# Two layer normalisations moved to ScalarE in the first phase of an attention and FFN block, with new instruction orders

## The reference

```python
mod = (silu(c) @ wmod).reshape(8, 6, 1, 256); sa, ca, ga, sb, cb, gb = ...
ga, gb = sign-preserving max(|g|, 0.25)
h = layernorm(x) * (1 + ca) + sa                 # (x - mean) / sqrt(var + 1e-5)
q, k = phi(h @ Wq.T + bq), phi(h @ Wk.T + bk)    # phi = elu + 1;  v = h @ Wv.T + bv
# causal linear attention, 16 heads of 16, for each token t:
#   num_t = q_t . sum_{s<=t} k_s v_s^T ;  den_t = q_t . sum_{s<=t} k_s + 1e-6
x = x + ga * ((num / den) @ Wo.T + bo)
h = layernorm(x) * (1 + cb) + sb
x = x + gb * ffn_block(h)     # two layers: windowed attention with rotary embedding, then a gated GELU FFN
```

## Time and profile before

| | us |
|---|---|
| median of 3 runs | 3326.53 |
| lowest, highest | 3323.44, 3328.26 |
| the profiled execution | 3325.04 |
| its span | 3323.2 |
| PE busy | 3176.3 (96%) |
| DVE busy | 2807.2 (84%) |
| POOL busy | 2515.7 (76%) |
| ACT busy | 2068.8 (62%) |
| granted TensorE clock, mean | 0.988 |

### The profile page before, as it was taken

How to read it: one execution, slowest core, us unless ns; L and a number is a source line. 1 busy time by engine, 2 the same in 40 slices (tenths; PEclk the granted TensorE clock), 3 DMA queues, 4 the chain that set the end, 5 groups by cost and what they waited for, 6 DMA issues and landing times.

```text
span 3323.2 us, 84307 instructions
## 1 busy us (share of the span) xinstructions
PE 3176.3 (96%) x25436; PEld 2433.4 (73%) x25436; DVE 2807.2 (84%) x8628; ACT 2068.8 (62%) x5116; POOL 2515.7 (76%) x2636
## 2 busy tenths in 40 slices
PE   5999999789999999999999999999999999999998
PEld 3666666457777777777777777777777777777777
DVE  5999999678888888888888888888888888888885
ACT  3555555346666666666666666666666666666664
POOL 3888888677777776777677777887878787878785
PEclk8999999889999999999999999999999999999999
DMA  6211111100000000000000001111111111111110
GB/s 223 68 45 43 44 44 43 37 15 24 24 24 24 24 24 24 24 24 23 24 24 24 24 25 34 36 37 37 36 37 36 37 38 35 38 35 40 34 42 30
DMA packets 153068, 124.98 MB, mean 38 GB/s; under 512 B 22580, under 2 KB 149032, under 8 KB 152368
## 3 DMA queue, kind: packets, MB, share of 16 engines
q1 hardware_dynamic: 146352, 110.67, 10.9%
q10 hardware_dynamic: 6272, 8.93, 0.9%
HBM read 77.51 MB, written 42.02 MB: 36 GB/s over the span
## 4 chain that ended last, share of the span: by engine, by line
PE 75%; DVE 12%; issue 8%; POOL 2%; ACT 1%; DVEq 1%; DMA 0%; SPq 0%; POOLq 0%; ACTq 0%
PE bank L540 26%; PE bank L736 17%; PE bank L744 10%; PE bank L547 7%; PE bank L709 7%; PE bank L688 5%; DVE shared L1055 2%; DVE a_den L1044 1%; DVE a_den L1042 1%; DVE z L1010 1%; DVE a_moments L999 1%; DVE a_moments L1075 1%; DVE shared L1036 1%; DVE gated L1070 1%; DVEq L362 1%
## 5 line engine op out<-in xcount | busy, mean ns | idle before, releaser
L540 PE MATMUL bank<-WQKV,xT 128*128 128x512 f32 x1536 | 745.9, 609 | 4.9 <-DVE rotary_work L1109 4.4
L1301 POOL TENSOR_TENSOR rnorm<-clamped,HALF 128x8 f32<-128x8 f32 x256 | 420.4, 1642 | 431.0 <-DVE clamped L1126 430.8
L736 PEld LDWEIGHTS bank<-zT,W 128*128 128x128 f32 x5632 | 661.6, 193 | 61.9 <-issue 59.6
L736 PE MATMUL bank<-zT,W 128*128 128x128 f32 x5632 | 673.8, 276 | 1.8 <-ACT zT L919 1.8
L1314 POOL TENSOR_TENSOR shared<-shared,share_of 128x512 f32<-128x512 f32 x512 | 543.6, 1080 | 89.9 <-DVE shared L1161 89.9
L905 ACT ACTIVATE shared<-shared,negmax 128x256 f32<-128x256 f32 x1024 | 507.4, 499 | 25.4 <-DVE negmax L1145 23.8
L540 PEld LDWEIGHTS bank<-WQKV,xT 128*128 128x128 f32 x1536 | 264.4, 192 | 215.3 <-issue 214.5
L1324 POOL TENSOR_TENSOR shared<-shared,IDENT 128x256 f32<-128x256 f32 x512 | 377.5, 757 | 0.0
L1308 POOL TENSOR_TENSOR qk<-qk,rnorm 128x512 f32<-128x512 f32 x256 | 289.1, 1129 | 103.7 <-DVE qk L1116 93.7
L1145 DVE CUSTOM_DVE_ANT_0 shared<-bank,MASK 128x256 f32<-128x256 f32 x1024 | 365.7, 419 | 0.1
L744 PEld LDWEIGHTS bank<-W,shared 128*128 128x128 f32 x1280 | 243.0, 190 | 90.8 <-issue 58.8
(11 more groups left out here) (141 smaller groups left out, 6788.8 us busy)
## 6 DMA issues: line engine op xcount, KB each, us to landing
X<-xl_rows SPq DMA_DIRECT2D x128, 128.0 KB, 2.2
X<-in_x SPq DMA_DIRECT2D x64, 128.0 KB, 2.1
x_tiles<-ax SPq DMA_DIRECT2D x64, 128.0 KB, 1.7
xl_rows<-axl SPq DMA_DIRECT2D x64, 128.0 KB, 1.7
XS<-xl_rows SPq DMA_DIRECT2D x128, 64.0 KB, 2.4
xm_rows<-X SPq DMA_DIRECT2D x128, 64.0 KB, 1.6
xs<-xm_rows SPq DMA_DIRECT2D x128, 64.0 KB, 1.8
xl_rows<-X SPq DMA_DIRECT2D x64, 128.0 KB, 1.7
```

The lines of the kernel that those rows point to most:

```text
L540: mm = nc.tensor.matmul(held(tile, key)[:, 0:cols], lhsT[c], rhs[c], start=(c == 0), stop=(c == len(lhsT) - 1))
L736: mm = nc.tensor.matmul(held(tile, key)[:, k * P:(k + 1) * P], W1[:, tile.l, c, at:at + P], zT[:, c], start=(c == 0), stop=(c == KC - 1))
L1301: G.tensor_tensor(rnorm[q][:], clamped[q][:], HALF[:].to_broadcast((P, LH)), ALU.pow).then_inc(done[f"root_{key}"], 1)
```

## The change

Both normalisations of phase A go from DVE (`tensor_scalar`: subtract, multiply) to ACT, as Identity with scale rstd and offset -mean * rstd. POOL computes that offset in `a_root`: it multiplies the mean by -1, raises the variance to -0.5 as before, waits for that, and multiplies the two. So the step gives two signals a tile instead of one. The epsilon 1e-6 of `a_queries` is added as a tensor of 16 equal elements instead of a scalar. Two constants are filled at the start. The orders of all five engines in phase A and the PSUM banks of phase A are new; phase L's are not changed.

```diff
 ORDER_A = {
-    "SP": [(0, "a_modulation"), (0, "a_load"), (4, "a_keep_x1"), (5, "a_store")],
-    "PE": [(2, "a_project_v"), (1, "a_project"), (2, "a_turn_q"), (3, "a_number"), (2, "a_sum"), (2, "a_score"), (3, "a_out"),
-           (0, "a_turn_z"), (1, "a_cum")],
-    "ACT": [(2, "a_keep_kphi"), (2, "a_keep_cum"), (2, "a_keep_q"), (3, "a_keep_o"), (1, "a_exp"), (2, "a_copy0"),
-           (2, "a_copy1"), (0, "a_affine")],
-    "DVE": [(2, "a_prod"), (2, "a_queries"), (4, "a_stats2"), (2, "a_value"), (0, "a_stats"), (1, "a_bias"), (4, "a_norm2"),
-           (0, "a_norm"), (2, "a_state"), (1, "a_phi"), (2, "a_mask2"), (2, "a_mask3"), (3, "a_gate")],
-    "POOL": [(4, "a_x1"), (5, "a_mod"), (4, "a_root2"), (0, "a_root"), (3, "a_add_state"), (0, "a_pre"), (2, "a_mask0"),
-           (2, "a_mask1")],
+    "SP": [(0, "a_modulation"), (0, "a_load"), (5, "a_store"), (4, "a_keep_x1")],
+    "PE": [(2, "a_cum"), (1, "a_project"), (4, "a_out"), (2, "a_turn_q"), (2, "a_sum"), (3, "a_number"), (2, "a_score"),
+           (0, "a_turn_z"), (1, "a_project_v")],
+    "ACT": [(3, "a_copy0"), (3, "a_copy1"), (2, "a_keep_kphi"), (5, "a_norm2"), (2, "a_keep_cum"), (2, "a_keep_q"),
+           (0, "a_norm"), (1, "a_exp"), (3, "a_keep_o"), (0, "a_affine")],
+    "DVE": [(3, "a_mask3"), (2, "a_value"), (2, "a_prod"), (2, "a_queries"), (0, "a_stats"), (1, "a_bias"), (4, "a_gate"),
+           (2, "a_state"), (4, "a_stats2"), (1, "a_phi"), (2, "a_mask2")],
+    "POOL": [(3, "a_mask0"), (3, "a_mask1"), (5, "a_mod"), (0, "a_root"), (4, "a_x1"), (0, "a_pre"), (4, "a_root2"),
+           (3, "a_add_state")],
 }
...
+            def a_norm(tile):                                       # on ACT
+                after(act, done["a_root"], tile, per=2)
+                after(act, filled["az"], tile, back=1)
+                nc.scalar.activation(az[:], xin[tile.s][:], ACT.Identity, scale=a_rstd[0][:], bias=a_offset[0][:]).then_inc(done["a_norm"], 1)
+            def a_norm2(tile):                                      # on ACT
+                after(act, done["a_root2"], tile, per=2)
...
+                nc.scalar.activation(axl[tile.s % 2][:], ax1[tile.s % 2][:], ACT.Identity, scale=a_rstd[1][:],
+                                     bias=a_offset[1][:]).then_inc(done["a_norm2"], 1)
...
-            def a_norm(tile):                                       # on DVE
...
-                V.tensor_scalar(az[:], xin[tile.s][:], a_meanvar[0][:, 0:1], a_rstd[0][:], ALU.subtract, ALU.mult).then_inc(done["a_norm"], 1)
...
-                V.tensor_scalar(a_den[:], a_den[:], EPS_DEN, None, ALU.add).then_inc(done["a_den"], 1)
+                V.tensor_tensor(a_den[:], a_den[:], EPSD[:], ALU.add).then_inc(done["a_den"], 1)
...
-            def a_norm2(tile):                                      # on DVE
...
-                V.tensor_scalar(axl[tile.s % 2][:], ax1[tile.s % 2][:], a_meanvar[1][:, 0:1], a_rstd[1][:], ALU.subtract,
-                                ALU.mult).then_inc(done["a_norm2"], 1)
...
             def a_root(k, tile):                                    # on POOL, for both normalisations
...
+                G.tensor_tensor(a_offset[k][:], a_meanvar[k][:, 0:1], MINUS[:], ALU.mult)
                 G.tensor_tensor(a_rstd[k][:], a_variance[k][:], HALF[:], ALU.pow).then_inc(done[("a_root", "a_root2")[k]], 1)
+                after(pool, done[("a_root", "a_root2")[k]], tile, per=2, ahead=-1)
+                G.tensor_tensor(a_offset[k][:], a_offset[k][:], a_rstd[k][:], ALU.mult).then_inc(done[("a_root", "a_root2")[k]], 1)
```

More of the change, by code:

```diff
@@ L81 @@
 BANK_A = {
-    "av": "20410305", "aqk": "63752641", "aq": "41031020", "num": "26475375", "kv": "63752641", "sc0": "04103752",
-    "sc1": "75264263", "sc2": "16375374", "sc3": "20410105", "awo": "10314204", "az": "16375265", "kphi": "75264763",
-    "cum": "16375224",
+    "kphi": "13041305", "cum": "26262616", "aqk": "30413042", "awo": "30413041", "aq": "57575747", "kv": "30413251",
+    "num": "26265626", "sc2": "75757674", "sc3": "13041305", "sc0": "26262416", "sc1": "04130723", "az": "30413042",
+    "av": "75757554",
 }
@@ L236, in adaln_block @@
         ZERO = sb("ZERO", [P, 1])
+        MINUS = sb("MINUS", [P, 1])
         modT = sb("modT", [P, B, 2 * KC])
@@ L246, in adaln_block @@
         a_variance, a_rstd = several(2, "a_variance", [P, 1]), several(2, "a_rstd", [P, 1])
+        a_offset = several(2, "a_offset", [P, 1])
+        EPSD = sb("EPSD", [P, AH])
         a_den, a_rden = sb("a_den", [P, AH]), sb("a_rden", [P, AH])
@@ L807, in _ @@
             last_project_a = {"a_project": "aqk", "a_project_v": "av"}[latest(ORDER_A["PE"], ["a_project", "a_project_v"])]
+            def a_norm(tile):
[4 more added lines that the diff above has]
+                after(act, done["a_root2"], tile, per=2)
+                if tile.least >= 2:
+                    n = (tile.s - 2) // STREAMS + 1
+                    act.wait_ge(stored[(tile.s - 2) % STREAMS], tile.at.block * (U * 4) + 16 * n)
+                nc.scalar.activation(axl[tile.s % 2][:], ax1[tile.s % 2][:], ACT.Identity, scale=a_rstd[1][:],
+                                     bias=a_offset[1][:]).then_inc(done["a_norm2"], 1)
             def a_affine(tile):
@@ L854, in a_keep_o @@
                 copy(flat(oaT), held(tile, "num")[:, 0:D]).then_inc(done["a_keep_o"], 1)
-            run_tiles(act, "A", ORDER_A["ACT"], {"a_affine": a_affine, "a_exp": a_exp, "a_keep_kphi": a_keep_kphi, "a_keep_cum": a_keep_cum,
+            run_tiles(act, "A", ORDER_A["ACT"], {"a_norm": a_norm, "a_norm2": a_norm2, "a_affine": a_affine, "a_exp": a_exp, "a_keep_kphi": a_keep_kphi, "a_keep_cum": a_keep_cum,
                                                  "a_keep_q": a_keep_q, "a_keep_o": a_keep_o,
@@ L952, in _ @@
             V.memset(HALF[:], -0.5).then_inc(consts_ready, 1)
+            V.memset(MINUS[:], -1.0).then_inc(consts_ready, 1)
+            V.memset(EPSD[:], EPS_DEN).then_inc(consts_ready, 1)
             V.memset(zeros, 0.0).then_inc(consts_ready, 1)
@@ L1003, in a_stats @@
                 after(dve, done["a_variance"], tile, per=3, ahead=-1)
-                after(dve, done["a_root"], tile, back=1)
+                after(dve, done["a_root"], tile, back=1, per=2)
                 V.tensor_scalar(a_variance[k][:], a_meanvar[k][:, 1:2], EPS_LN, None, ALU.add).then_inc(done["a_variance"], 1)
-            def a_norm(tile):
-                after(dve, done["a_root"], tile)
-                after(dve, filled["az"], tile, back=1)
-                V.tensor_scalar(az[:], xin[tile.s][:], a_meanvar[0][:, 0:1], a_rstd[0][:], ALU.subtract, ALU.mult).then_inc(done["a_norm"], 1)
             def a_bias(tile):
@@ L1079, in a_stats2 @@
                 after(dve, done["a_variance2"], tile, per=3, ahead=-1)
-                after(dve, done["a_root2"], tile, back=1)
+                after(dve, done["a_root2"], tile, back=1, per=2)
                 V.tensor_scalar(a_variance[1][:], a_meanvar[1][:, 1:2], EPS_LN, None, ALU.add).then_inc(done["a_variance2"], 1)
-            def a_norm2(tile):
[L1084 to L1087, removed]
-                V.tensor_scalar(axl[tile.s % 2][:], ax1[tile.s % 2][:], a_meanvar[1][:, 0:1], a_rstd[1][:], ALU.subtract,
-                                ALU.mult).then_inc(done["a_norm2"], 1)
-            steps = {"a_stats": a_stats, "a_norm": a_norm, "a_bias": a_bias, "a_value": a_value, "a_phi": a_phi, "a_prod": a_prod,
-                     "a_queries": a_queries, "a_state": a_state, "a_gate": a_gate, "a_stats2": a_stats2, "a_norm2": a_norm2}
+            steps = {"a_stats": a_stats, "a_bias": a_bias, "a_value": a_value, "a_phi": a_phi, "a_prod": a_prod,
+                     "a_queries": a_queries, "a_state": a_state, "a_gate": a_gate, "a_stats2": a_stats2}
             steps.update({f"a_mask{g}": partial(a_mask, g) for g in range(COPIED, GROUPS)})
```

2 lines of the change are left out of this document (1 added, 1 removed).

## The result

The changed kernel is slower: 3339.19 us (median of 6 runs, 3335.42 to 3341.40) against 3324.97 (6 runs of the kernel before, 3323.24 to 3328.26). The ratio is 1.0041, interval 1.0030 to 1.0052. The profiled execution took 3339.53 us, span 3337.7; that is 14.5 us over the span of before, at the same clock (0.987 and 0.988). Forecast were 3316 us.

What follows compares the result with a forecast made beforehand. PE and DVE were level at 9.03 us a tile in phase A, PE's own work 8.49. From 3325.04 us, 60 x (8.85 - 9.03) + 1.5 = -9.3 gave 3315.7, say 3316; range 3294 to 3338.

Steps and rivals of the forecast that it cites:

- A gate-to-gate period of 8.85 us: Phase A: the time from one tile's gate to the next was to fall from 9.03 to 8.85 us.
- well under 95%: Sign for 200 to 500 us: DVE busy well under 95%, with POOL over 92% and ACT near 70%.
- The small product: Each of four new one-element POOL products a tile was taken at 0.15 us from start to start.
- the 0.25 that I named as a sign of being wrong: The prediction called itself wrong if a one-element POOL product took over 0.25 us.
- POOL's case as a rival: Rival, chance 0.22: POOL becomes the bound; with 0.25 us a small product the period is 9.3 and the time 3343 us.
- The pause of PE at the turn of the queries: Phase A: PE waits 0 to 0.6 us a tile for the queries; half, 0.3, was taken, giving 8.8.
- just covered: `a_phi` was not to wait: `a_exp` ends some 3.2 us after the queries' turn, DVE's other work lasts about 3.5.
- 8.7 us of work and 0.2 of waiting a tile: POOL in phase A: 7.89 us own work plus 0.53 and 0.27 held by DVE, two idle waits of 0.1, giving 8.9.
- the epsilon at 0: L1044 as a tensor addition still waits for POOL: gain 0, bounds 0 and 0.57 us.
- the 1.37 us at four places, phase L (orders unchanged) and the DMAs [...] I cost at 0: Extra time where the program changes loop copies, phase L and the DMAs were all taken as unchanged, cost 0.
- POOL's slot without the rotary factors: POOL's per-tile sum in phase A: 7.05 us, 7.89 with new products and waits, 8.7 with what DVE holds.
- The filling and emptying at +1.5 (0 to 3): Phase A pipeline: `a_out` and `a_gate` a tile further back add a partly filled slot at the end, +1.5 us.

Runs made afterwards that it cites:

- experiment 9: Changed kernel with rotary factors multiplied before the first tile and 32 instructions of met waits in DVE's straight code between phase A's loops: 3323.47 us, ratio 0.9999.
- experiment 7: Changed kernel without POOL's two small offset products per root, ACT normalising with offset 0: 3324.54 us in a single run.
- Experiment 5: Kernel before with only the denominator's epsilon added as a tensor of 16 elements: 3324.31 us against 3324.03, ratio 1.0001.
- experiment 3: Changed kernel with met waits making 32 instructions on DVE ahead of its phase A: 3333.18 us, ratio 1.0024.
- 4: Changed kernel with met waits making 64 instructions on DVE ahead of its phase A: 3333.78 us, ratio 1.0030.
- experiment 2: Changed kernel with POOL multiplying the eight rotary factors before the first tile, not one by one in eight tiles: 3332.35 us, ratio 1.0024.
- experiment 1: Changed kernel with ACT issuing phase L's weight loads ahead of the first normalisation, not behind the affine step: 3337.85 us, ratio 1.0036.
- 10: Changed kernel with factors first, met waits between the loops, and the offset computed on ACT in place of POOL: 3325.28 us, ratio 1.0005.
- 8: Changed kernel with rotary factors first and met waits making 80 instructions on DVE ahead of its first tile: 3332.99 us, ratio 1.0024.
- 6: Changed kernel's new instructions in the kernel before's orders and banks, both normalisations on ACT ahead of the exponential: 3361.24 us, ratio 1.0105.
- 11: Changed kernel with rotary factors first and the product with -1 made by DVE ahead of the variance: 3324.53 us, ratio 0.9998.
- 12: Changed kernel with factors first, product with -1 on DVE, and 116 instructions of met waits in tiles 0 to 3: 3315.05 us, ratio 0.9969.

## Why the prediction was wrong

**Right: the slot and what bounds it.** "A gate-to-gate period of 8.85 us": 8.89 in undisturbed stretches. DVE was to be well under 95% and was 81%; POOL over 92%, and was 90% in a stretch that holds a hole (91.8% in experiment 9, which has none), a little short; ACT near 70%, and was 65%. The normalisations take 0.60 us each on ACT, where I took 0.55. The small product takes 0.19 us as reported and 0.14 from start to start (569.11 to 569.25 in POOL's timeline) where nothing holds it; 0.15 was taken. The first product's mean, 256 ns, is over the 0.25 that I named as a sign of being wrong; it comes from the 8 of 65 that wait out a DVE instruction (0.69 to 0.74 us; at 571.93 one takes 0.73, beside `a_phi`), and the other 57 are as forecast. POOL's case as a rival, a period of 9.3, didn't occur; the four products cost 0.14 a tile, by experiment 7.

The pause of PE at the turn of the queries was taken at 0.3 us a tile. PE's waits in the changed kernel, 200 to 500 us (us in total, times, longest), give 9.6 / 33 = 0.29, and another 0.17 for `a_phi`, which I had as just covered:

```profile
PE bank L550 <- DVE shared L1064: 9.6, 25, 0.8
PE bank L586 <- DVE LATE L1045: 5.6, 16, 0.6
```

POOL's part of the period is partly luck. I had 8.7 us of work and 0.2 of waiting a tile, 0.80 of the work for what DVE holds (0.53 and 0.27, which no row shows). In experiment 9 POOL is busy 275.6 of 300 us, 8.2 a tile, and idle 0.7: less work and more waiting, with nearly the same sum.

**Right: the epsilon at 0.** Experiment 5 measured 706 ns against 709. So by these rows the form with one SBUF input is held as well as the one with two.

**Wrong: what was costed at 0.** The step that failed is the one that read "the 1.37 us at four places, phase L (orders unchanged) and the DMAs [...] I cost at 0". I had seen the four places and taken them as a property of the loop. They are a property of where its code lies and how long it is. The change made DVE's body shorter (313 instructions in place of 352) and moved it: two jumps became free and two went to 4.5 us, which with the slower restart of PE cost 11.5 us. Against the 5.5 of before that is +6.0. Experiments 3 and 4 show it: they add nothing but met waits, and the holes went and came. Experiment 9 adds them to experiment 2, which by itself had kept both holes (4.38 and 4.25), and they went.

**Wrong: POOL's slot without the rotary factors.** I summed what POOL does in every tile, and left out what it does in eight of them, 1.28 us each. A slot in which POOL has room hides that; the change took the room, and the sum had to be made again for those tiles. By experiment 2 it is 6.8 us of the time.

**Wrong: the filling and emptying at +1.5 (0 to 3).** Experiment 9 is free of holes and factors, so it isolates the term. From the start to the first load of phase L it needs 630.23 us, 5.0 less than before. The slots alone would give 60 x (8.89 - 9.03) = -8.4, and the four jumps -5.5, together -13.9; so the filling and emptying cost about +9 net. I had also put the term at the end, and it lies at the start: the gate of tile 8 comes 9.8 us later than before (142.85 against 133.01), and from the gate of tile 56 to the first load of phase L it takes 2.6 us less (60.30 against 62.90). How much of it is the depth itself and how much ACT's DMA issues in the first eight tiles, stays open; experiment 1 moved those and got 1.1 us.

Phase L changed by +1.8 us, inside the 3 that were allowed. The sum with the measured terms, of the profiled executions: slots -8.4; jumps +6.0; the filling and emptying +8.9; phase L +1.8; and the factors +5.5, taken against experiment 9 like the filling (start to gate of tile 8: 146.00 against 142.85; tiles 24 to 40: 144.95 against 142.59). That is +13.8 where +14.5 was measured. Experiment 2 itself puts the factors at 9.3 in its gates and 6.8 in the medians; two single executions of the same code differ by 1.7 us up to the gate of tile 8 (141.16 and 142.85), and experiment 9's profiled execution (3318.42 us) is the fastest of its eleven, 5.1 under their median; so each term is good to some us only. What I can't put to a row is the split of the filling.

**What the holes are.** The trace also records instruction packets, the pieces of code that come in by DMA: 8192 bytes each on queue 14 (but for a few small ones), 16384 each on queue 8. The DMA queues (packets, MB, share) over one pass of the second loop, 464 to 541.5 us, and over a pass and a half of the first, 182 to 309 us, both of the changed kernel:

```profile
q1 hardware_dynamic: 3456, 3.15, 12.6%
q14 instruction: 5, 0.04, 0.2%
```

```profile
q1 hardware_dynamic: 6160, 5.61, 13.5%
```

The loop with holes brings in five pieces in every pass; the loop without holes brings in none. It is so for every loop in phase A of all fourteen kernels. At the jump after 464.37 three pieces start at 464.25, 466.92 and 469.39 us, and the hole lasts from 464.37 to 468.91. So DVE waits for its own code. (The record names the queue of a packet, not its engine; that these are DVE's is read from their coming with DVE's holes and from nothing else.)

**The rule of the Trainium skill that bears on it** is in Runtime: NRT & Kernel Launch, section "Instruction fetch mechanics": a taken branch to code outside the window that an engine holds must fetch that code first. The trace agrees, by these packets. The page gives no size; in phase A it is 1.5 to 4.7 us. With start and length of each loop counted in DVE instructions, from the start of the first loop of the changed kernel, the runs give:

```
kernel or experiment        start  length  pieces  holes, us
changed kernel, 1, 2, 7        0     313      3    none (9 and 10 too)
                             595     313      4    4.2 to 4.7
3                             32     313      4    2.8, 2.7
3, 9, 10                     627     313      3    none
4                             64     313      4    2.2, 2.2
                             659     313      3    none
8                             80     313      4    4.6, 4.1
                             675     313      4    2.6, 2.8
6                         4, 598     312      3    none
11                            12     329      4    3.3, 3.3
                             639     329      3    none
12                      128, 755     329      3    none
before                        23     352      4    1.9, 1.8
                             689     352      4    1.5, 1.5
5                        24, 690     352      4    1.6, 1.6; 1.8, 1.6
```

The start alone gives no simple rule: in experiment 6 a loop at 598 is free, and at 595 one stalls 4.5 us. The column "pieces" does. It cuts the code into pieces of 128 instructions, with a border 44 instructions before the zero of this count: a loop that lies in three pieces runs free, one that reaches into a fourth has a hole at each jump. I fitted the 44; but no other size of piece up to 599 instructions, with any border and any limit on their number, gives all these loops, except 129. The longest holes (starts 595 and 80) are those where the loop begins in the last four instructions of a piece; there the next piece is needed almost at once, which would explain their length but wasn't tested by itself. That the pieces are loaded at the jumps is shown; the rule of three pieces is read from these runs afterwards, and none was made to test it.

## What to carry to other kernels

Before pricing a reordering, sum the engine that will be tightest over the tiles with extra work as well, not over the ordinary slot alone. Treat each idle time that the profile puts down to "issue" at a loop's jump as changeable by any edit of that engine's code: count it after the change, look for instruction packets there, and if it has grown, move or shorten the loop so that it lies in fewer pieces. Here moving the factors and one loop was worth 15.7 us, beside a change whose slot gained 8.4.

## What the hardware showed that I had not expected

The same jump of DVE costs nothing or 4.6 us, by where the loop's code begins and ends. In phase L the same kind of hole stands at the jumps in all kernels (14 idle times put down to "issue", 53.9 us before and 53.5 after, up to 5.05 each). The waits of experiments 3, 4, 8, 9 and 12 moved that code too, and the sum stayed at 52.9 to 55.5 us. Its loops have 737 instructions, more than three pieces hold, so the rule above expects holes there at every place.

What one hole costs depends on PE's clock. Where the granted clock stays at 1.00, the interval grows by less than the hole: 2.1 us for 2.8 (experiment 3), 3.3 for 4.07 (experiment 8, its stretch from 255 to 260 us below). Where it falls, as to 0.55 between 470 and 475 us in the changed kernel, mostly the lower of its two levels (1.2 GHz in place of 2.4), the interval after the jump is long as well (11.42 and 10.31), and two holes of 4.54 and 4.57 cost 6.3 and 5.2.

```profile
255.00:260.00 5.00, 2.99 (x38) 2.42 (x42) 4.52 (x14) 1.50 (x5) 1.25 (x4) 1.00 0.08 28
```

A POOL product of one element a partition costs 0.19 us alone and 0.73 when it meets `a_phi` on DVE. So what it costs a kernel depends on which instruction it meets.
